# A list schedule for one core: the tie between ready operations is broken by the oldest batch item, not by the longest way of operations to the end

## The reference, cut to what matters

```python
h = _layernorm(x) * (1 + ca) + sa
x = x + ga * attn(h, Wq, Wk, Wv, Wo, rel_emb)            # attention 1: relative position bias
h = _layernorm(x) * (1 + cb) + sb
# the ffn part:
h2 = h + _attention(_rmsnorm(h, g1), wq, wk, wv, wo)      # attention 2: rotary, causal
y = h2 + _moe(_rmsnorm(h2, g2), w_router, wg, wu, wd)     # 8 experts, top 2, hidden size 384
x = x + gb * y
```

## Time and profile before

| | |
|---|---|
| median of 3 runs | 1042.7 us (1042.02 to 1046.67) |
| profiled execution, its own time | 1047.42 us |
| span in its profile | 1045.6 us (1.8 us less than its time) |
| busy: PE, DVE, ACT, POOL | 889.1, 695.8, 517.1, 199.4 us |
| mean granted TensorE clock | 0.932 of full speed |

### The profile page before, as it was taken

How to read it: one execution, slowest core, us unless ns; L and a number is a source line. 1 busy time by engine, 2 the same in 40 slices (tenths; PEclk the granted TensorE clock), 3 DMA queues, 4 the chain that set the end, 5 groups by cost and what they waited for, 6 DMA issues and landing times.

```text
span 1045.6 us, 36360 instructions
## 1 busy us (share of the span) xinstructions
PE 889.1 (85%) x15358; PEld 552.5 (53%) x15358; DVE 695.8 (67%) x1504; ACT 517.1 (49%) x876; POOL 199.4 (19%) x246
## 2 busy tenths in 40 slices
PE   4678888798999999989998799999889888889921
PEld 2334454455545555545544455555457577789910
DVE  1553665848586978667866877787676765567843
ACT  1246355373736565636565166556455444445500
POOL 1250020000111022020211200020212210022475
PEclk9899899898989999989999699999899999999975
DMA  8358630000000000000000100000011122233443
GB/s 214 160 185 316 227 108 2 8 8 1 24 8 14 16 13 23 3 22 13 18 19 17 31 13 13 3 18 18 12 32 33 40 65 62 60 91 100 134 122 88
DMA packets 52782, 61.50 MB, mean 59 GB/s; under 512 B 5584, under 2 KB 39376, under 8 KB 52240
## 3 DMA queue, kind: packets, MB, share of 16 engines
q1 hardware_dynamic: 38256, 29.81, 9.3%
q10 hardware_dynamic: 10272, 20.97, 5.4%
q0 software_dynamic: 4096, 8.40, 2.8%
HBM read 23.71 MB, written 35.45 MB: 57 GB/s over the span
## 4 chain that ended last, share of the span: by engine, by line
PE 55%; DVE 24%; issue 9%; ACT 6%; POOL 5%; DMA 1%; SPq 0%; POOLq 0%; DVEq 0%; ACTq 0%
DVE row_max L1147 15%; PE ps L815 9%; PE ps L704 6%; PE ps L671 5%; PE ps L898 5%; PE ps L716 4%; POOL eo_g L1430 4%; PE ps L652 3%; PE ps L890 2%; PE ps L646 2%; PE ps L682 2%; PE ps L892 2%; PE ps L891 2%; ACT stage L941 2%; ACT k_head L941 2%
## 5 line engine op out<-in xcount | busy, mean ns | idle before, releaser
L1147 DVE TENSOR_REDUCE row_max<-ps 128x4 f32<-128x1024 f32 (+1 forms) x256 | 265.9, 1080 | 39.9 <-PE ps L682 26.0
L997 ACT ACTIVATE probs<-ps 128x1024 f32<-128x1024 f32 x128 | 130.2, 1028 | 85.8 <-PE ps L704 83.7
L997 ACT ACTIVATE stage<-ps 128x1024 f32<-128x1024 f32 x96 | 98.1, 1025 | 85.7 <-PE ps L710 84.8
L671 PE MATMUL ps<-bias_t,ch 64*32 64x512 f16 x2048 | 109.3, 402 | 20.7 <-DVE row_max L1147 14.2
L1384 POOL TENSOR_TENSOR rstd_n<-var_n,cf 128x2 f32<-128x2 f32 x48 | 34.3, 716 | 369.0 <-DVE var_n L1084 368.7
L890 PE MATMUL ps<-xT_t,wgu_hi 128*128 128x256 f16 x276 | 76.1, 276 | 15.8 <-DVE hid L1318 11.0
L1313 DVE SCALAR_TENSOR_TENSOR gate_s<-gate_t,ps 128x256 f32<-128x256 f32 x138 | 57.5, 417 | 44.6 <-ACT gate_t L1042 44.5
L1415 POOL DMA_INDIRECT slot_rows<-rows,slots x64 | 64.4, 1006 | 117.4 <-DVE slots L1259 103.1
L1430 POOL DMA_INDIRECT eo_g<-slot_rows,slots x64 | 60.8, 950 | 124.0 <-DMA slot_rows<-eo_t 76.8
L815 PE MATMUL ps<-probs,v_pad 128*32 128x256 f32 x1024 | 82.3, 395 | 0.5 <-ACT probs L997 0.3
L1042 ACT ACTIVATE gate_t<-ps 128x256 f32<-128x256 f32 x138 | 53.0, 384 | 58.0 <-PE ps L892 54.5
(11 more groups left out here) (166 smaller groups left out, 1669.7 us busy)
## 6 DMA issues: line engine op xcount, KB each, us to landing
slot_rows<-gate_s ACTq DMA_DIRECT2D x1, 12544.0 KB, 36.7
slot_rows<-gate_s ACTq DMA_DIRECT2D x1, 7936.0 KB, 24.1
x_t<-slot_rows SPq DMA_DIRECT2D x46, 128.0 KB
slot_rows<-eo_t SPq DMA_DIRECT2D x46, 128.0 KB
xT<-in_x SPq DMA_DIRECT2D x16, 128.0 KB, 2.2
kept<-resid SPq DMA_DIRECT2D x16, 128.0 KB, 1.7
resid_b<-kept SPq DMA_DIRECT2D x16, 128.0 KB, 2.2
out_dram<-outT SPq DMA_DIRECT2D x16, 128.0 KB
```

The source lines that it names most:

```text
L671: eng.matmul(ps[HR * c:HR * (c + 1), lo + r, :].rearrange("p (j s) -> p j s", j=2), csth("flip")[half, :], bias_t[half, way, 2 * g:2 * g + ...
L997: eng.activation(probs[a][:, 2 * (k % 2):2 * (k % 2) + 2, :], ps[:, lo:lo + 2, :], ACT.Exp).then_inc(z["exp"], 1)
L1147: ins = eng.tensor_reduce(row_max[a][:, qt, 4 * g:4 * g + 4].rearrange("p (r j) -> p r j", r=2), of_heads, AX.X, ALU.max)
```

## The change

`line(key)` is the tie break in `Plan.run`. Before, fronts, cores, ends and hand-overs of all items but item 0 were in one class, ordered by `-way[key]`: `way` is the sum of estimated durations and hops along the longest chain of operations from this one to the end of the kernel. Tiles and final pieces ("moe") came behind them, ordered among each other by their own `way`. Now the attention's operations are ordered by `key[1]`, the item's number, and inside an item by the order in which the jobs were listed. "moe" still comes behind, ordered by `key[1]`, the piece's number; all final pieces have higher numbers than all tiles. The computation of `way` goes. Operations, waits, durations in the plan and tile sizes stay as they are.

```diff
-        def step(key):
-            eng, us = self.ops[key][0:2]
-            return us + HOP[eng] if eng else us
-
-        open_ = dict(waits)
-        order = [k for k, n in waits.items() if not n]
-        for k in order:
-            for n in then.get(k, ()):
-                open_[n] -= 1
-                if not open_[n]:
-                    order.append(n)
-        way = {}
-        for k in reversed(order):
-            way[k] = step(k) + max([way[n] for n in then.get(k, ())], default=0.0)
-
         def line(key):
-            if key[0] == "moe":
-                return (2, -way[key], rank[key])
-            return (1 if key[1] else 0, -way[key], rank[key])
+            return (1, key[1], 0) if key[0] == "moe" else (0, key[1], rank[key])
```

## The result

| | before | after |
|---|---|---|
| median | 1042.7 us (5 runs) | 1114.46 us (5 runs, 1113.27 to 1120.03) |
| profiled execution, its own time | 1047.42 us | 1120.03 us |
| span in its profile | 1045.6 us | 1118.2 us |
| mean granted TensorE clock | 0.932 | 0.902 |

The ratio after/before is 1.0685, with a 95% interval of 1.0648 to 1.0723. The kernel became 71.8 us slower by the medians; the forecast was 62.6 us, a median of 1105.

What follows compares the result with a forecast made beforehand. PE was taken as the engine to keep fed, held up mostly by DVE. Attention +79.9, fewer tiles behind it -39.6 and -1.3, later gathers +23.6 make +62.6 us: 1042.7 becomes 1105.3 us, range 1079 to 1131.

Steps and rivals of the forecast that it cites:

- "tok" 15: Hand-over of item 15, the end of attention: predicted to start at 921.6 us instead of 841.7, 79.9 us later.
- "tok" 15 to the last "dn": Tiles left between item 15's hand-over and the last tile's "dn" matmuls: 115.9 us predicted instead of 156.8.
- gather 17 against the last "dn": POOL's first gather for item 4, relative to the last tile's "dn" matmuls: predicted to start 23.6 us later.
- end behind gather 17: From the first gather for item 4 to the kernel's end: the same 66.6 us predicted to follow.
- Step 3: Final pieces: acc of item 2 stands behind the last tile, so item 4's gathers start later, +23.6 us.
- Step 2: Behind attention: nine tiles fewer, -39.6 us, and transposes of six items' final pieces gone from the tiles, -1.3 us.
- Step 1: Attention, oldest item first: fewer begun younger items fill PE's gaps, PE 85.7% busy, item 15's hand-over 79.9 us later.
- The rival of the falling clock: Attention: more gaps lower PE's clock and lengthen matmuls; at a share of 80% the median is 1167 us; chance 0.08.
- A stock of begun younger items is what fills this: Attention: begun younger items fill PE's waits when both cores stand in DVE or ACT steps; the new order keeps fewer.
- The count by weight loads: Attention: weight-load busy time instead of matmuls, 46.5% share, item 15's hand-over at 988, kernel 1172 us; inside a chance of 0.08.
- The order is of no account: Attention: PE stays 90.4% busy whatever the order, item 15's hand-over at 876.3, median 1060 us; chance 0.11.
- the other side: Attention: oldest item first removes waits, PE 92.9% busy, item 15's hand-over at 854.1, median 1037.8 us; chance 0.04.

Runs made afterwards that it cites:

- e1: Kernel before with only attention reordered, oldest item first; tiles and final pieces still by way: 1095.19 us, ratio 1.0493.
- e2: Kernel before with only tiles and final pieces reordered, by number; attention still by way: 1063.59 us beside 1043.55, ratio 1.0202.
- e4: Kernel before without classes: tiles and final pieces compete with attention, longest way first: 1039.67 us, ratio 0.9959.
- e3: Kernel before with attention oldest item first, but fronts and core 1 counted four items older; the rest by way: 1137.40 us, ratio 1.0899.
- e7: Kernel before with attention oldest first, but cores behind, lower step number first; tiles by way: 1029.48 us, ratio 0.9869; rerun in a later set 1117.68 us, ratio 1.0036.
- e8: Kernel before with attention oldest first, cores in a class behind, oldest item first among them too; tiles by way: 1098.68 us, ratio 1.0544.
- e12: Kernel before with all attention jobs in one class, ordered by the operation's number inside its job; second run of that kernel: 1123.00 us, ratio 1.0086.
- e5: Kernel before with the bias matmuls ahead of attention 1's scores issued twice, 1024 matmuls more: 1056.79 us beside 1043.09, ratio 1.0128.
- e6: Changed kernel with the bias matmuls ahead of attention 1's scores issued twice, 1024 matmuls more: 1119.86 us, ratio 1.0719 to the kernel before.
- e10: Kernel before with all jobs in one class, longest way first, plus small shifts of way for each kind of job: 1066.93 us, ratio 0.9598.

## Why the prediction was right, and where it was not

**Sign and size.** 1114.5 us lies inside 1079 to 1131 and 9.5 us from the 1105 forecast. The terms came out as follows.

| term | predicted | measured |
|---|---|---|
| "tok" 15 | +79.9 | +94.2 |
| "tok" 15 to the last "dn" | -40.9 | -43.2 |
| gather 17 against the last "dn" | +23.6 | +21.4 |
| end behind gather 17 | 0 | +0.2 |
| span | +62.6 | +72.6 |

**Step 3 was right**, in mechanism and nearly in size. The listing had put the acc of item 2 behind the last `hid`. There it was, with 46.5 us of waiting for it (48 predicted) and the same 66 to 67 us behind it. e1 and e2 take the term apart from the rest: 19.3 and 20.0 us. It is 2.2 us smaller than predicted since the transposes of items 0 and 1 ran ahead of the last "dn", at 1048.81, and not behind it.

**Step 2 was right.** 16 tiles were ahead of "tok" 15, and 30 took 113.6 us (115.9 predicted). "dn" started 4.4 us apart again:

```profile
965.75 1.55 PE L880 MATMUL ps<-wd,hid 128*128 x12
970.16 1.54 PE L880 MATMUL ps<-wd,hid 128*128 x12
```

By these sizes, moving nine tiles ahead of "tok" 15 is no loss (31.5 us there, 39.6 given back behind it), and e4, which has 16 more there and gains 4 us, is in line with that.

**Step 1 had the right row of numbers for the wrong reason, and was mis-sized by 14.3 us.** The share of busy PE wasn't the 85.7% that I had chosen but 776.6 / 885.9 = 87.7%; by itself that would have brought "tok" 15 sooner, at 50 + 747.0 / 0.877 = 901.8. What failed is the sentence "The work is the same, so only idle time can grow or shrink". The matmuls are the same, but the busy time that they take is not: 803.0 us and not 772.7. The mean clock up to "tok" 15 gives most of the reason. With two levels, 1.2 and 2.4 GHz, a mean of 0.94 over 841.7 us is (1 - 0.94) x 2 x 841.7 = 101 us at the lower one, and 0.92 over 935.9 us is 150 us, 49 us more (the mean is rounded, so each within 9 us). At half rate PE does in 49 us what takes 24.5 at full, so by this estimate the clock accounts for at most about 25 of the 30.3 us, with 9 either way; whether the rest is the clock too, these rows can't tell. A single matmul shows the cost directly: in the kernel before, one of L704 with 256 columns takes 269 ns where the granted clock is 1.00 (350 to 390 us) and up to 418 ns where it is 0.50 (114 to 124 us). The rival of the falling clock was therefore not another case but a part of this one, and I had given it a chance instead of a term. At the share of 87.7%, an estimate that lets only gaps change would have missed by 34 us. The guess of 85.7% was too low by 2 points, which hid 20 of these 34 us, and steps 2 and 3 came out 4.5 us better than forecast: that the total came within 10 us is luck in part.

**The mechanism in step 1 was wrong.** "A stock of begun younger items is what fills this": e3 has the stock of before and is 94 us slower than before. And e7, with the small stock of the changed kernel, is 85 us faster than that by the medians. What the runs showed in its place is the rule between the two attentions' cores: e7 against e8 shows that this rule alone is worth 69 us in the same classes. That it acts through the overlap of the two is argued from the table, not shown. The number of cores in flight doesn't account for it: e7 has about 1.5, (46.6 + 30.9) x 16 in some 820 us, slightly less than before, and is faster, and e12 has 1.72 and isn't. Even advance is what e7 was made for, and it was measured as a whole; that evenness acts through the clock is read from the stretches, not tested by itself.

**The count by weight loads** in step 1 (the Trainium skill, "Trainium Kernel Development and Optimization", Performance Expectations) would have led to 1172 us. The page says this of how close a kernel is to roofline, the best that the chip could do, and names the share of the peak rate reached beside the weight loads; that a time can be forecast by them is my use of it. Busy weight loads from 50 us to "tok" 15 turned out as 446.5 / 885.9 = 50.4% of the time, not the 46.5% that a third of the way gave. With the measured share of each, the weight loads put "tok" 15 at 50 + (407.5 + 28.8) / 0.504 = 916 and the busy matmuls at 902, and the trace has it at 936. So by itself the count was no worse a measure than mine; what failed in it was taking a third of the way between its two ends. The rows of the clock bear out "TensorE: Matmul & The Clock Gate", Part 1, of the Trainium skill: idle PE is throttled, here to a mean clock of 0.79 in a stretch of e3 with 34% gaps. e5 and e6 show the reverse, work in the gaps that gives time back.

**The other rivals.** "The order is of no account" would have been 1060 us, and the other side 1037.8: neither. But e7 shows that the other side wasn't empty. In the set of e7, an order by the oldest item was 1.3% faster than the longest way with the cores left out of it; in the later set it was 0.4% slower.

## What to carry to other kernels

When a change only reorders the work of an engine that is some 85 to 90% busy, cost the gaps and the clock both: the same matmuls took 30 us more here, up to 25 of them by estimate because PE was at 1.2 GHz for longer. In a list schedule the tie break decides which chains run side by side, so look at whether one of them wins every tie, and not at how many are begun or how many are in flight on average. Read the end of the kernel by itself: one add placed behind the last tile instead of five ahead cost 20 us, since a queue with a fixed pace stood behind it.

## What the runs showed that was not expected

- 1024 matmuls added to attention, 28 us of PE's work, made the kernel before 13.7 us slower and the changed one about 4 us (0 to 11). PE's busy time grew by 18.3 and 7.0 us, and the mean granted clock rose by 0.014 and 0.021.
- The same kernel took 1043 us in three sets of runs and 1112.0 and 1115.4 us in two later ones, with a spread of under 1% in each. Of e7, profiled in both, row maxima kept their length. Half of the 60 us lost up to "tok" 15 were waits between engines, and half busy PE at a lower mean clock.
- These circumstances change which order is better: e7 went from 0.987 to 1.004 of the kernel before. e10, measured only in the first of the two later sets, was at 0.960; how it does in the others isn't known.
